# Decoder layer: self attention by query chunk, stack loads into 96 partitions, and zero products at three borders

## What is computed

```python
# self attention, 16 heads of width 16
q, k = _apply_rope(proj(WQ_w, WQ_b)), _apply_rope(proj(WK_w, WK_b));  v = proj(WV_w, WV_b)
scores = jnp.where(causal, q @ k.T / sqrt(16), -inf)
x = _layernorm(x + softmax(scores) @ v @ Wo_w.T + Wo_b)
# cross attention: each token picks the nearest of 1601 context rows, attends to the picked rows
qp = x @ Wq.T;  idx = argmax(qp @ kv.T);  mem = kv[idx]
mk, mv = split(mem @ Wkv.T)
x = _layernorm(x + softmax(qh @ mk.T / 4) @ mv @ Wc.T)
# 8 experts (four of width 256, four of width 512), the top two by sigmoid gate
topw, sel = top_k(sigmoid(x @ router_w.T), 2);  topw = topw / topw.sum(-1)
x = _layernorm(x + sum(topw[e] * (relu(x @ W1[e]) ** 2 @ W2[e]) for e in sel))
```

## Time and profile before

| what | us |
|---|---|
| median of 3 runs (lowest, highest) | 1178.02 (1176.01, 1183.33) |
| the profiled execution, its own time | 1180.42 |
| its span, first to last instruction | 1178.7 |
| TensorE busy in the span | 1031.4 |
| VectorE, ScalarE, GpSimd busy | 873.4, 591.1, 289.1 |
| mean granted TensorE clock | 0.928 |

### The profile page before, as it was taken

One profiled execution on the slowest core, in us unless ns is written; L12 is line 12 of the kernel. 1 busy time (PEld: TensorE's weight loads), 2 busy tenths in 40 slices (PEclk: granted clock), 3 DMA queues, 4 the chain that ended last, 5 costly groups with the idle time before them and its releaser, 6 DMA issues. The chain is left out here.

```text
span 1178.7 us, 17913 instructions
## 1 busy us (share of the span) xinstructions
PE 1031.4 (88%) x6184; PEld 508.8 (43%) x6184; DVE 873.4 (74%) x1770; ACT 591.1 (50%) x819; POOL 289.1 (25%) x268
## 2 busy tenths in 40 slices
PE   6869999999999999988989779989898869889960
...
GB/s 184 164 125 29 77 77 62 61 133 29 39 2 1 1 1 2 1 1 31 54 28 38 1 105 152 64 24 68 14 64 29 37 30 42 70 139 69 72 92 162
DMA packets 60825, 70.04 MB, mean 59 GB/s; under 512 B 10364, under 2 KB 53756, under 8 KB 60732
## 3 DMA queue, kind: packets, MB, share of 16 engines
...
## 5 line engine op out<-in xcount | busy, mean ns | idle before, releaser
L608 DVE TENSOR_REDUCE piece_max<-self_banks 128x1 f32<-128x512 f32 (+3 forms) x640 | 349.8, 603 | 47.7 <-PE self_banks L473 28.1
L555 ACT ACTIVATE early<-self_banks 128x1024 f32<-128x1024 f32 (+3 forms) x320 | 274.3, 896 | 175.5 <-PE self_banks L491 174.5
L1696 DVE TENSOR_REDUCE cross_piece_max<-banks 128x1 f32<-128x512 f32 x256 | 163.9, 683 | 32.4 <-PE banks L1586 31.3
L1668 ACT ACTIVATE cross_probs<-banks 128x1024 f32<-128x1024 f32 x128 | 126.5, 1023 | 100.3 <-PE banks L1609 98.5
L501 PE MATMUL self_banks<-early,V 128*17 128x512 f32 (+3 forms) x1280 | 149.9, 540 | 2.6 <-ACT early L555 2.0
L430 POOL TENSOR_SCALAR_AFFINE_SELECT early<-early 128x512 f32<-128x512 f32 x64 | 40.8, 637 | 370.8 <-ACT early L555 370.5
L473 PE MATMUL self_banks<-stack_k,stack_q 96*128 96x512 bf16 (+3 forms) x320 | 108.5, 381 | 9.7 <-DVE piece_max L608 6.0
L1586 PE MATMUL banks<-kx_few,stackx 97*128 97x512 bf16 x256 | 97.5, 421 | 17.4 <-DVE cross_piece_max L1696 8.8
L473 PE MATMUL self_banks<-late 96*128 96x512 bf16 (+3 forms) x320 | 102.6, 356 | 2.0 <-DVE piece_max L608 0.9
L491 PE MATMUL self_banks<-late 98*128 98x512 bf16 (+3 forms) x320 | 87.0, 353 | 2.8 <-DMA late<-shift 2.8
L491 PE MATMUL self_banks<-stack_q,stack_k 98*128 98x512 bf16 (+3 forms) x320 | 84.9, 353 | 3.5 <-DMA stack_q<-shift 2.2
...
## 6 DMA issues: line engine op xcount, KB each, us to landing
...
```

The lines of the kernel that those rows point to most:

```text
L555: nc.scalar.activation(probs[:, i % 3, 2 * pair:2 * pair + 2, st["off"]:C], ps[:, 2 * pair:2 * pair + 2, st["off"]:C], ACT.Exp, scale=SCAL ...
L608: nc.vector.tensor_reduce(piece_max[:, u % 2, pc["row"], pc["at"]:pc["at"] + 1], slot[:, 0:pc["w"]], AX.X, ALU.max).then_inc(side_read, 1)
L1668: nc.scalar.activation(probs[:, i % 3, 2 * pair:2 * pair + 2], ps[:, 2 * pair:2 * pair + 2], ACT.Exp, scale=SCALE).then_inc(probs_ready, 1)
L1696: nc.vector.tensor_reduce(piece_max[:, u % 2, pc["row"], pc["at"]:pc["at"] + 1], slot[:, 0:pc["w"]], AX.X, ALU.max).then_inc(side_read, 1)
```

## The change

1. The DRAM tensors hold all six rows of the stack ready, q and k duplicated per pair; a unit's parts go out in three DMAs (`RUNS`), 6 rows of 1 KB per partition. `PAIRS` is in another order for that.
2. A stack now holds all 16 heads of one chunk, and a load is one DMA into 96 partitions for q and one for k. Loads: chunk 0 heads 0 to 3, chunk 0 heads 4 to 15, chunks 1, 2 and 3.
3. The loop goes chunk by chunk, and within one over the head groups. `schedule` is as it was. The maximum over a unit's pieces reads only the slots that its chunk fills.
4. `split_extras` and `add_bias` run at units 12 and 13, and their loads on SP move with them.
5. `zero_products` multiplies 128 x 128 zeros on TensorE: 6 times ahead of the last sums of the self attention, 8 times more at the start of the cross attention and once after each piece ahead of its steps (21), and 24 times ahead of the experts' first turn.
6. Each expert's row carries x: the gates are doubled (the sum of the two is halved before its reciprocal), and y = gate times expert output, plus x. The two rows then add up to twice the residual sum, whose layer norm is the same with 4 times the epsilon. The additions on GpSimd go, each chunk has a semaphore of its own, and VectorE adds the two gathered rows.

```diff
-PAIRS = [(0, 0), (0, 1), (1, 0), (0, 2), (2, 0), (1, 1)]
+PAIRS = [(0, 0), (1, 0), (2, 0), (0, 1), (1, 1), (0, 2)]
+RUNS = [(0, 3), (3, 2), (5, 1)]
...
+    def zero_products(bank, times):
+
+        for n in range(times):
+            nc.tensor.matmul(bank[:, 0:P], zeros[:], zeros[:], start=True, stop=True)
...
-        qparts = nc.dram_tensor("qparts", [3, D, T], BF16).ap()
-        kparts = nc.dram_tensor("kparts", [3, D, T], BF16).ap()
+        qparts = nc.dram_tensor("qparts", [P, len(PAIRS), KD, T], BF16).ap()
+        kparts = nc.dram_tensor("kparts", [P, len(PAIRS), KD, T], BF16).ap()
...
-            last_q = late[:, 28 * C + 44:36 * C + 44].bitcast(BF16)
-            stack_q = [sb(att, "stack_q0", [P, NC, GH, C], BF16)]
-            stack_q += [rows.rearrange("p (c h t) -> p c h t", c=NC, h=GH) for rows in (halves(16), last_q)] + stack_q
-            stack_k = [sb(att, "stack_k0", [P, GH, T], BF16)]
-            stack_k += [rows.rearrange("p (h t) -> p h t", h=GH) for rows in (halves(0), halves(8))] + stack_k
+            def heads_of(rows):
+                return rows.rearrange("p (h t) -> p h t", h=H)
+
+            stack_q = [sb(att, "stack_q0", [P, H, C], BF16), heads_of(halves(16))]
+            stack_k = [sb(att, "stack_k0", [P, H, C], BF16), heads_of(halves(0)), heads_of(halves(8)),
+                       heads_of(late[:, 28 * C + 44:36 * C + 44].bitcast(BF16))]
...
-            def stack_pairs(g, c0, c1):
-                pairs = []
-                heads = slice(g * GH * DK, (g + 1) * GH * DK)
-                cols = slice(c0 * C, c1 * C)
-                for n, (a, b) in enumerate(PAIRS):
-                    rows = slice(n * DK, (n + 1) * DK)
-                    for c in range(c0, c1):
-                        pairs.append((stack_q[g][rows, c], qparts[a, heads, c * C:(c + 1) * C].rearrange("(h i) t -> i h t", i=DK)))
-                    pairs.append((stack_k[g][rows, :, cols], kparts[b, heads, cols].rearrange("(h i) t -> i h t", i=DK)))
-                return pairs
+            def stack_pairs(c, h0, h1):
+                half = DK // KD
+                return [(to[0:KS, h0:h1], there[h0 * half:h1 * half, :, :, c * C:(c + 1) * C].rearrange("(h i) s m t -> (i s m) h t", i=half))
+                        for to, there in ((stack_q[c % 2], qparts), (stack_k[c], kparts))]
...
-            loads = [stack_pairs(0, c, c + 1) for c in range(NC)] + [stack_pairs(g, 0, NC) for g in range(1, NG)]
+            loads = [stack_pairs(0, 0, GH), stack_pairs(0, GH, H)] + [stack_pairs(c, 0, H) for c in range(1, NC)]
             steps, works = [], []
-            chunks = [(g, c) for g in range(NG) for c in (range(NC) if g < NG - 1 else range(NC)[::-1])]
+            chunks = [(g, c) for c in range(NC) for g in range(NG)]
...
+                            pieces.append(dict(w=b - a, lhsT=stack_q[c % 2][0:KS, g * GH + j, q * P:(q + 1) * P],
+                                               rhs=stack_k[n][0:KS, g * GH + j, 0:b - a], row=j * GH + q, at=n,
+                                               diag=b == end, load=c + 2 if c or g else 1))
+                works.append(dict(pieces=pieces, slots=c + 1,
...
-            extra_work = {7: split_extras, 11: add_bias}
+            extra_work = {NC * NG - 4: split_extras, NC * NG - 3: add_bias}
...
-                        dst = (qparts, kparts)[t].rearrange("r (p m) t -> m p r t", m=KD)[m, :, :, c * C:(c + 1) * C]
                         if n == len(units) - KD:
                             send_shift(0)
-                            sp.wait_ge(s_parts_out[(NC - 2) % 2], 16 * TC * (NC // 2))
-                            load(NC - 2)
                         sp.wait_ge(p3_ready, n + 1)
-                        sp.dma_start(dst, parts[:, n % SLOTS]).then_inc(s_parts_out[c % 2], 16)
-                        if 0 < c < NC - 1 and n % 4:
-                            if n % 4 == 1:
-                                sp.wait_ge(s_parts_out[(c - 1) % 2], 16 * TC * ((c + 1) // 2))
-                            for to, there in loads[c - 1][(n % 4 - 1) * 4:n % 4 * 4]:
-                                sp.dma_start(to, there).then_inc(s_load[c - 1], 16)
+                        for b, (s, many) in enumerate(RUNS):
+                            sp.dma_start((qparts, kparts)[t][:, s:s + many, m, c * C:(c + 1) * C],
+                                         parts[:, n % SLOTS, b:b + 1].to_broadcast([P, many, C]) if t else parts[:, n % SLOTS, 0:many]
+                                         ).then_inc(s_parts_out[c % 2], 16)
+                        if n in (5, 9):
+                            sp.wait_ge(s_parts_out[0], 16 * len(RUNS) * TC)
+                            load((n - 5) // 4)
...
                         if u == 1:
-                            for i in range(2):
-                                sp.wait_ge(s_parts_out[i], 8 * len(units))
-                            load(NC - 1)
-                        if u in (2, 3):
-                            load(u + 2)
-                        if u == 5:
-                            sp.wait_ge(probs_used, first_of[NC])
-                            load(NC + 2)
-                        if u == 6:
+                            sp.wait_ge(s_parts_out[1], 16 * len(RUNS) * TC)
+                            load(2)
+                        if u == NG + 1:
+                            sp.wait_ge(s_parts_out[0], 8 * len(RUNS) * len(units))
+                            sp.wait_ge(probs_used, first_of[NG])
+                            load(3)
+                        if u == 2 * NG + 1:
+                            sp.wait_ge(s_parts_out[1], 8 * len(RUNS) * len(units))
+                            sp.wait_ge(probs_used, first_of[2 * NG])
+                            load(4)
+                        if u == 2 * NG + 2:
                             for dst, there in extras:
...
+                            if st["unit"] == 2 * NG:
+                                for r in range(2):
+                                    pool.wait_ge(s_parts_out[r], 8 * len(RUNS) * len(units))
...
+                        if i == len(steps):
+                            zero_products(ps[:, 0], 6)
...
-                                    act.wait_ge(s_parts_out[n // 4 % 2], 16 * TC * (n // SLOTS))
+                                    act.wait_ge(s_parts_out[n // 4 % 2], 16 * len(RUNS) * TC * (n // SLOTS))
...
-                        link(nc.vector.tensor_scalar_add(total[:], total[:], 1e-20))
+                        link(nc.vector.tensor_scalar(total[:], total[:], 1e-20, 0.5, ALU.add, ALU.mult))
...
+                            zero_products(po, 2 * C // P)
...
+                                if item[0] == "piece":
+                                    zero_products(po, 1)
...
-            s_yb = [sem(f"yb_in{i}") for i in range(3)]
-            yb_need = [(0, 64), (0, 64), (1, 32), (2, 32)]
+            s_yb = [sem(f"yb_in{c}") for c in range(NC)]
...
-                    def added(c):
-                        pool.wait_ge(s_yb[yb_need[c][0]], yb_need[c][1])
-                        mine = second[:, TC * c:TC * (c + 1)]
-                        nc.gpsimd.tensor_tensor(mine, mine, o_tok[:, TC * c:TC * (c + 1)], ALU.add).then_inc(first_added, 1)
...
-                    added(0)
                     for c in range(NC):
-                        if c + 1 < NC:
-                            added(c + 1)
                         root(c)
...
+                    zero_products(px, 6 * C // P)
...
-                        nc.vector.tensor_scalar(ys[:, i % YR], py[:, 0:D], xin[:, i % XR, D:D + 1], None, ALU.mult).then_inc(y_read, 1)
+                        nc.vector.scalar_tensor_tensor(out=ys[:, i % YR], in0=py[:, 0:D], scalar=xin[:, i % XR, D:D + 1], in1=xin[:, i % XR, 0:D],
+                                                       op0=ALU.mult, op1=ALU.add).then_inc(y_read, 1)
...
-                        dve.wait_ge(first_added, c + 1)
-                        mine = x_sb[:, TC * c:TC * (c + 1)]
-                        link(nc.vector.tensor_tensor(mine, mine, second[:, TC * c:TC * (c + 1)], ALU.add))
+                        mine = slice(TC * c, TC * (c + 1))
+                        dve.wait_ge(s_yb[c], 32)
+                        link(nc.vector.tensor_tensor(x_sb[:, mine], o_tok[:, mine], second[:, mine], ALU.add))
...
-                        nc.vector.tensor_scalar_add(rstd[:, TC * c:TC * (c + 1)], mv[:, TC * c:TC * (c + 1), 1], EPS).then_inc(var_ready, 1)
+                        nc.vector.tensor_scalar_add(rstd[:, TC * c:TC * (c + 1)], mv[:, TC * c:TC * (c + 1), 1], 4 * EPS).then_inc(var_ready, 1)
```

38 lines of the change are left out of this document (17 added, 21 removed).

## The result

The median of the changed kernel is **1169.86 us** (1166.48 to 1170.59), a ratio of 0.9917 with an interval of 0.9889 to 0.9946. The forecast was 1151.0 with a range of 1144 to 1166: the sign is right, the gain is 8.2 us instead of 27. The profiled execution has a span of 1168.8 us (1178.7 before), so its 9.9 us can be accounted for stage by stage.

The account below looks back on a forecast made before the run. Self attention was taken as bound by VectorE's maxima, then TensorE, then ScalarE's exponentials, plus late transfers. Self attention -17, borders -1.5, tail -9.8, front queue +1.3 gave -27: 1151.0 us from 1178.0, range 1144 to 1166.

Parts of the forecast that it names:

- The front: Projection units, 28 to 75 us: doubled stores hidden under VectorE, 0; first shift DMA may queue up to 2 us, +1.3.
- The rate of a load into 96 partitions: Stack loads: taken as 350 GB/s, with 111 kept for the range; chunk 1's load would land near 95 us.
- The self attention's order: Self attention, 75 to 532 us: chunk by chunk, same work, 440 us against 457.2, 17 us less.
- The borders: Zero products at three stage borders: together -1.5 us.
- The first: Border from self attention to search: 6 zero products, transposes at full clock, -1 us (from +0.5 to -1.2).
- The second: Border from search to cross attention: 12 zero products and one after each of 21 pieces, +0.5 us (-1.5 to +4).
- The third: Border from cross attention to experts: 24 zero products before the first turn, taken as -1 us.
- the clock falls first: Cross attention to experts: zeros start at half clock, end at 970.4, experts' first products at 977.2; 0 gain.
- The tail: After the experts, 1140 us to the end: VectorE adds the gathered rows without GpSimd, -9.8 us (-12 to -6).
- Rival B: Self attention loop: the order only moves dry steps and half clock elsewhere, 0 there, tail -9.8: 1168 us; chance 0.10.
- My own list of signs: Prediction wrong if TensorE waits for a chunk 0 stack load, chunk 0 exceeds 65 us, or stores stretch pairs past 6.41.
- C: Front and chunk 0: new transfers run at the slow rate both ways, slower kernel, 1249 us at 111 GB/s; chance 0.05.

Follow-up runs that it names:

- e9: Changed kernel with chunk 3's stores behind the first loads and shift rows on SP's queue, and 7 zero products ahead of the experts: 1151.92 us, ratio 0.9776.
- e11: Changed kernel with its stack loads cut into DMAs of four heads each: 1164.31 us, ratio 0.9902.
- e5: Kernel of e4 with unit 0's two shift rows sent from ScalarE's queue instead of SP's: 1161.43 us, ratio 0.9872.
- e4: Changed kernel with chunk 1's load ahead of unit 1's shift rows on SP's queue: 1169.27 us, ratio 0.9891.
- e10: Kernel of e9 without the 6 zero products ahead of the self attention's last sums: 1157.13 us, ratio 0.982.
- e12: Kernel of e9 with the stack loads cut by four heads as in e11: 1155.24 us, ratio 0.9818.
- e1: Kernel before with only the tail's change (rows that carry x, VectorE's own addition, a semaphore per chunk): 1172.82 us, ratio 0.9915.
- e7: Kernel of e5 with 7 zero products instead of 24 ahead of the experts' first turn: 1158.86 us, ratio 0.9861.
- c1: The kernel before, unaltered, profiled again: span 1177.3 us.

## Why the prediction was wrong

1. **The front was taken at 0, plus 1.3 for a queue of at most 2 us: the step that failed.** The sum asked whether a pair's stores (4.5 us of DMA) fit under VectorE's 6.41 us, and they do: the maxima were on time. It added the two loads that run among them at the rate of the stores, 41 us of DMA out of 47. An estimate with the measured rates: 3.1 MB of loads at about 210 GB/s take 15 us, not 9, and with 31 for the stores the 47 us are full. They were: the DMA share was 1.00 to 1.15 from 50 to 80 us. Measured: +4.65 us where the sum had +1.3. e9 took it away with data moved behind the shift rows, e11 took 2.45 us of it with faster loads, and e5, by another queue, only the part that was a late issue.
2. **The rate of a load into 96 partitions was taken as 350 GB/s**, "nearer to 128" than to 16. It was 207. Chunk 1's load, whose shift rows came at 90.1 instead of 85, was needed at 104.5 and landed at 109.2 (at 350 GB/s, by the forecast's own 9 us, it would have landed near 101); wait and half clock cost 6.0 us (e4). With point 1 that is 10.7 us.
3. **The self attention's order was right.** Its four chunks were forecast at 440 us. With neither wait, e9 took 443.3 us: 58.3, 95.6, 130.1 and 159.4 against 58, 94, 129.5 and 158.6 (444.5 and 445.0 in e10 and e12). Of the 17 us forecast 12 to 13 are there, and 4.5 of these are the half clock behind the wait of the earlier trace rows, which e1 did not pay in the old order.
4. **The borders were taken at -1.5 and came to +1.1.** The first gave -0.4 for -1: the 16 transposes at full clock took 2.45 us where the sum had 1.7. The second gave -0.3 for +0.5. The third cost 1.8 for -1. I had the case "the clock falls first" and priced it at 0. The zeros of it ended nearly as worked out (11.4 us behind the last sums, here 12.0), but the experts' first products behind them took 8.1 us (967.84 to 975.94) where I had 6.8. I weighed both cases alike, by one trace in which the clock held for 4 us of this border; in the next it fell within 2 us of the last sums, over 2 us before the zeros began. And less than a third of their number gains what all were to gain (e7).
5. **The tail was right**: -9.8 forecast, -10.2 measured, each step of it (1149.4 for the first addition: 1149.34; 3.27 us a chunk: 3.31).
6. **Not in the sum: the 39 tiles**, 1.7 us longer. The pace of the later ones is the same, but in two stretches, with a wait of 2.8 us for VectorE's `hT_rest` and one of 4.2 for the rows of `xin` (3.3 before), the clock was 0.77 against 0.89 before. By e7 and c1 the new code is not the cause:

```profile
1020.00:1035.00 15.00, 12.23 (x67) 10.95 (x68) 9.31 (x24) 3.74 (x9) 9.20 (x10) 0.77 0.31 106
1050.00:1065.00 15.00, 13.21 (x73) 11.82 (x74) 5.96 (x11) 3.94 (x8) 2.87 (x3) 0.77 0.23 64
```

Rival B had the right figure, 1168, by luck, and not the mechanism: the loop does what it says, and the front takes it back. My own list of signs had it: TensorE waited for a stack load in chunk 0 (4.7 us), and chunk 0 took 64.8 us, just short of the 65 that the list names. The chance of that stood with C alone, at the extreme price of 111 GB/s, and not with a case between.
